# A Mamba branch beside a two-layer local-attention branch on one core: dt by one Softplus activation, and the rotary addition by an accumulating DMA that GpSimd issues

## The reference, cut to what matters

```python
def mamba(x):                                     # 512 inner channels, 16 states
    x_inner, z = split(x @ in_proj_w.T)
    x_conv = silu(causal_conv4(x_inner) + conv_b)
    dt_lr, B, C = split(x_conv @ x_proj_w.T)
    dt = softplus(dt_lr @ dt_proj_w.T + dt_proj_b)
    h_t = exp(dt_t * A) * h_(t-1) + (dt_t * x_conv_t) * B_t      # per channel and state
    y_t = sum_n h_t[n] * C_t[n] + x_conv_t * D
    return (y * silu(z)) @ out_proj_w.T

def attention_layer(x, l):                        # 2 layers, 8 heads of 64, windows of 128
    q, k, v = split(shift_token(x) @ wqkv[l])
    q, k = l2norm(q) * q_scale, l2norm(k) * k_scale
    q = q * cos * scale + rotate_half(q) * sin * scale
    k = k * cos / scale + rotate_half(k) * sin / scale
    x = x + local_attention(q, k, v) @ wo[l]
    return x + gelu_feed_forward(layernorm(shift_token(x)))
```

## Time and profile before

| | |
|---|---|
| median of 3 runs | 2244.7 us (2244.4 to 2245.45) |
| the profiled execution | 2240.7 us, its span 2238.9 us |
| PE busy | 2058.0 us (92%) |
| DVE busy | 2016.8 us (90%) |
| ACT busy | 1680.9 us (75%) |
| POOL busy | 928.2 us (41%) |
| DMA queues, share of 16 engines | q0 36.0%, q1 31.4% |
| mean granted TensorE clock | 0.976 |

### The profile page before, as it was taken

One profiled execution on the slowest core, in us unless ns is written; L12 is line 12 of the kernel. 1 busy time (PEld: TensorE's weight loads), 2 busy tenths in 40 slices (PEclk: granted clock), 3 DMA queues, 4 the chain that ended last, 5 costly groups with the idle time before them and its releaser, 6 DMA issues. The chain is left out here.

```text
span 2238.9 us, 37820 instructions
## 1 busy us (share of the span) xinstructions
PE 2058.0 (92%) x10944; PEld 1318.1 (59%) x10944; DVE 2016.8 (90%) x2804; ACT 1680.9 (75%) x4087; POOL 928.2 (41%) x1086
## 2 busy tenths in 40 slices
PE   6789989999899999999899998999989999898897
PEld 2355666656566566665566565666556656565565
DVE  2999989999899999999899998999989999899893
ACT  3777877968778787887778777787777868778682
POOL 2444343444434444443444433444443443533440
PEclk9889999999999999999999999999999999999999
DMA  4567767686676756877756876668667686667482
GB/s 142 145 152 194 188 155 183 180 205 175 161 196 178 188 161 157 220 187 169 193 136 189 208 187 165 157 179 200 181 166 196 173 197 167 163 162 217 115 200 54
DMA packets 113131, 388.52 MB, mean 174 GB/s; under 512 B 11408, under 2 KB 32272, under 8 KB 94368
## 3 DMA queue, kind: packets, MB, share of 16 engines
q0 software_dynamic: 46080, 151.02, 36.0%
q1 hardware_dynamic: 66848, 235.10, 31.4%
HBM read 238.75 MB, written 155.71 MB: 176 GB/s over the span
## 5 line engine op out<-in xcount | busy, mean ns | idle before, releaser
L756 DVE TENSOR_TENSOR_SCAN hb<-dA,state,hb 128x512 f32<-128x512 f32 x512 | 668.3, 1305 | 34.7 <-ACT dA L963 20.5
L1177 POOL COPY state<-hb 128x2 f32<-128x2 f32 x256 | 223.5, 873 | 638.5 <-DVE hb L756 638.2
L963 ACT ACTIVATE dA<-dt_sb,amat 128x512 f32<-128x512 f32 x512 | 344.3, 720 | 81.8 <-DMA ysum<-dA 80.8
L1193 POOL DMA_DIRECT2D ysum<-dA x256 | 220.2, 883 | 382.6 <-DVE dA L763 272.6
L1465 PE MATMUL ring<-hT,w 128*128 128x256 f32 (+1 forms) x1536 | 354.5, 388 | 17.4 <-ACT hT L1119 16.9
L1465 PEld LDWEIGHTS ring<-hT,w 128*128 128x128 f32 (+1 forms) x1536 | 272.6, 182 | 94.5 <-ACT hT L1119 26.0
L749 DVE TENSOR_TENSOR hb<-u_sb,bc 128x1024 f32<-128x1024 f32 x256 | 311.3, 1216 | 2.0 <-DMA bc<-bc_rows 1.9
L763 DVE TENSOR_TENSOR dA<-hb,bc 128x1024 f32<-128x1024 f32 x256 | 307.2, 1200 | 0.0
L1073 ACT ACTIVATE rot<-rot,rnorm 128x64 f32<-128x64 f32 x1024 | 257.2, 339 | 50.8 <-POOL rnorm L1262 50.7
L1098 ACT ACTIVATE probs<-ring,nmax 128x256 f32<-128x256 f32 x512 | 235.6, 483 | 55.5 <-DVE nmax L847 55.1
L1262 POOL TENSOR_TENSOR rnorm<-rnorm,powers 128x8 f32<-128x8 f32 x128 | 230.2, 1799 | 23.5 <-POOL rnorm L1259 23.5
(11 more groups left out here) (122 smaller groups left out, 3469.8 us busy)
## 6 DMA issues: line engine op xcount, KB each, us to landing
bc<-bc_rows SPq DMA_DIRECT2D x128, 1024.0 KB, 5.8
ysum<-dA POOLq DMA_DIRECT2D x256, 512.0 KB, 7.2
wqkv<-in_wqkv SPq DMA_DIRECT2D x48, 512.0 KB, 8.6
w<-in_w SPq DMA_DIRECT2D x16, 1364.0 KB, 9.5
...
wo<-in_wo SPq DMA_DIRECT2D x16, 512.0 KB, 10.0
...
```

Source lines behind the costliest of these rows:

```text
L756: dve.tensor_tensor_scan(hb[:, k % H_RING, :], dA[:, k % DA_RING, :], hb[:, k % H_RING, :], state[:, k:k + 1], ALU.mult, ALU.add).then_inc ...
L963: act.activation(dA[:, k % DA_RING, :], dt_sb[:, j, :], ACT.Exp, scale=amat[:, n:n + 1]).then_inc(dA_ready.sem, 1)
```

## The change

dt: the three activations and two VectorE operations become one activation, `Softplus`, from PSUM with the bias, straight into `dt_sb`; `clip` and `softplus(half)` are gone, and `u(half)` has only its product. The rotation: VectorE's addition at line 842 is gone, and a new stage `rot` on POOL issues a DMA from `sq` to `rot` (both in SBUF, 128 partitions by 2 KB, 256 KB) that adds to the destination. `norm_heads` and the next `square` wait for its landing. All order tables are written anew for it, of which two lines are shown.

```diff
 POOL_ORDER = """
...
-+scan +scan +turn(q,1) +q(2) +add(2) +add(3) +scan +scan +turn(k,1) +add(4) +add(5) +scan +add(6) +scan
...
+stats(3) +scan +skip(0) +scan +turn(q,1) +turn(k,1) +add(2) +scan +add(3) +scan +rot(q,1) +rot(k,1) +scan
...
-    rot_ready = Signal("rot_ready", 2 * NA)
+    rot_added = [Signal(f"rot_added_{x}", D16 * NA, primed=0) for x in "qk"]
...
             elif stage == "dt":
-                group(("dt", n[0]), (dtv_ready, n[0] + 1))
+                group(("dt", n[0]), (dt_ready, n[0] + 1))
...
-            def clip(half):
-                for j in range(half * JH, half * JH + JH):
-                    dve.wait_ge(*dtv_ready.at(it, j + 1))
-                    dve.wait_ge(*dBx_ready.at(it - 1, (half + 1) * SUMS // HALVES))
-                    dve.tensor_scalar(u_sb[:, j, :], dt_sb[:, j, :], 40.0, None, ALU.min).then_inc(dtmin_ready.sem, 1)
-
             def u(half):
 
-                for j in range(half * JH, half * JH + JH):
-                    dve.wait_ge(*dtlog_ready.at(it, j + 1))
-                    dve.tensor_tensor(dt_sb[:, j, :], dt_sb[:, j, :], u_sb[:, j, :], ALU.max)\
-                       .then_inc(dt_ready.sem, 1)
                 for j in range(half * JH, half * JH + JH):
                     dve.wait_ge(*dt_ready.at(it, j + 1))
                     dve.wait_ge(*xconv_ready.at(it, j + 1))
+                    dve.wait_ge(*dBx_ready.at(it - 1, (half + 1) * SUMS // HALVES))
                     dve.tensor_tensor(u_sb[:, j, :], dt_sb[:, j, :], xconv[:, j, :], ALU.mult).then_inc(u_ready.sem, 1)
...
-                dve.wait_ge(*sine_ready.at(it, n + 1))
-                dve.wait_ge(*rotary_ready.at(it, n + 1))
-                dve.tensor_tensor(rot[:, i, :], rot[:, i, :], sq[:, i, :], ALU.add).then_inc(rot_ready.sem, 1)
...
-            def dt_out(j):
+            def softplus(j):
                 act.wait_ge(*filled(it, ("dt", j)))
                 act.wait_ge(*dA_ready.at(it - 1, (j // JH + 1) * UNITS // HALVES))
-                act.activation(dt_sb[:, j, :], bank(it, ("dt", j))[:, :], ACT.Identity,
-                               bias=par[:, C_DTB + j:C_DTB + j + 1]).then_inc(dtv_ready.sem, 1)
-
-            def softplus(half):
-                act.preload_act_table_set("natural_log_exp_and_others")
-                for j in range(half * JH, half * JH + JH):
-                    act.wait_ge(*dtmin_ready.at(it, j + 1))
-                    act.activation(u_sb[:, j, :], u_sb[:, j, :], ACT.Exp).then_inc(dtexp_ready.sem, 1)
-                for j in range(half * JH, half * JH + JH):
-                    act.wait_ge(*dtexp_ready.at(it, j + 1))
-                    act.activation(u_sb[:, j, :], u_sb[:, j, :], ACT.Ln, bias=1.0).then_inc(dtlog_ready.sem, 1)
+                act.activation(dt_sb[:, j, :], bank(it, ("dt", j))[:, :], ACT.Softplus,
+                               bias=par[:, C_DTB + j:C_DTB + j + 1]).then_inc(dt_ready.sem, 1)
 
             def square(i, name, a):
                 n = 2 * a + i
-                act.wait_ge(*rot_ready.at(it, n - 1))
+                if it or a:
+                    act.wait_ge(*rot_added[i].at(it, D16 * a))
                 act.wait_ge(*filled(it, (name, a)))
                 act.activation(sq[:, i, :], bank(it, (name, a))[:, :], ACT.Square).then_inc(sq_ready.sem, 1)
...
-                act.wait_ge(*rot_ready.at(it, n + 1))
+                act.wait_ge(*rot_added[i].at(it, D16 * (a + 1)))
                 act.wait_ge(*rnorm_ready.at(it, n + 1))
...
+            def add_rotated(name, a):
+
+                i = "qk".index(name)
+                n = 2 * a + i
+                pool.wait_ge(*sine_ready.at(it, n + 1))
+                pool.wait_ge(*rotary_ready.at(it, n + 1))
+                pool.sem_inc(passed, 1)
+                pool.dma_start(rot[:, i, :], sq[:, i, :], accum_op=ALU.add).then_inc(rot_added[i].sem, D16)
+
```

More of the change, by code:

```diff
@@ L120 @@
++e(5,2) +e(5,3) +k(6) +dA +dA +dA +dA +pT(5,0) +pT(5,1) +v(5) +rb(5) +pT(5,2) +pT(5,3) +turn(q,6) +turn(k,6)
++dA +dA +heads(6) +v(6) +q(7) +hn(2) +e(6,0) +e(6,1) +hT(2) +e(6,2) +e(6,3) +last(2) +k(7) +pT(6,0)
+++skip(0) +dA +dA +pT(6,1) +dA +dA +dA +h(2,0) +h(2,1) +h(2,2) +h(2,3) +rb(6) +h(2,4) +h(2,5) +pT(6,2)
++pT(6,3) +turn(q,7) +turn(k,7) ++dA ++dA
 """
 POOL_ORDER = """
-add(30) add(31) scan +scan merge(1) +turn(q,0) +turn(k,0) +scan +q(1) +add(0) +add(1) stats(3) +skip(0)
-+scan +scan +turn(q,1) +q(2) +add(2) +add(3) +scan +scan +turn(k,1) +add(4) +add(5) +scan +add(6) +scan
@@ L175 @@
-e(5,2) e(5,3) v(5) rb(4) dA q(6) dA k(6) pT(5,0) pT(5,1) pT(5,2) pT(5,3) +softplus(0) rb(5) turn(q,6)
-turn(k,6) last(2) heads(6) v(6) dA dA dA dA e(6,0) e(6,1) hn(2) e(6,2) pT(6,0) e(6,3) q(7) pT(6,1) hT(2)
-pT(6,2) k(7) turn(q,7) h(2,0) h(2,1) dA dA pT(6,3) h(2,2) h(2,3) h(2,4) h(2,5) dA dA +dA +dA turn(k,7)
-+skip(0) rb(6)
+xn(0) xnT(0) start(0) xn(1) q(0) xnT(1) in(0) k(0) in(1) start(1) turn(q,0) +xn(0) in(2) in(3) turn(k,0)
+silu(0) silu(1) xdbl heads(0) v(0) dt(0) dt(1) dt(2) dA e(0,0) q(1) k(1) dA dA e(0,1) e(0,2) dA dA dA e(0,3)
@@ new lines @@
+pT(3,0) dA dA dA x2T(0) +in(1) +in(2) pT(3,1) pT(3,2) q(4) dA pT(3,3) dA dA +in(3) k(4) rb(3) +silu(0) dA dA
+turn(q,4) dA dA turn(k,4) hn(1) dA hT(1) +silu(1) q(5) k(5) heads(4) dA dA dA dA last(1) h(1,0) h(1,1)
+h(1,2) h(1,3) h(1,4) h(1,5) e(4,0) e(4,1) dA dA dA +xdbl pT(4,0) turn(q,5) dA +dt(0) +dt(1) pT(4,1)
+turn(k,5) v(4) dA heads(5) dA e(4,2) e(4,3) dA dA pT(4,2) x2T(1) e(5,0) e(5,1) e(5,2) e(5,3) q(6) k(6)
+pT(4,3) dA dA rb(4) v(5) pT(5,0) pT(5,1) pT(5,2) pT(5,3) rb(5) turn(q,6) turn(k,6) heads(6) dA dA e(6,0)
@@ new lines @@
+turn(k,2) add(2) scan scan add(3) add(4) scan add(5) scan q(3) add(6) add(7) rot(q,3) rot(k,3) scan
+turn(q,3) turn(k,3) add(8) stats(0) scan scan carry add(9) add(10) scan add(11) scan scan add(12) add(13)
++halo scan q(4) scan add(14) add(15) scan add(16) turn(q,4) add(17) rot(q,4) scan rot(k,4) merge(0)
+turn(k,4) skip(1) scan stats(1) q(5) scan scan add(18) add(19) add(20) add(21) rot(q,5) rot(k,5) scan scan
+turn(q,5) +tail turn(k,5) q(6) add(22) scan scan add(23) add(24) scan scan rot(q,6) rot(k,6) turn(q,6)
@@ L188 @@
+turn(k,6) add(25) add(26) q(7) stats(2) scan scan add(27) add(28) turn(q,7) scan rot(q,7) turn(k,7) rot(k,7)
+scan carry2 add(29) +q(0)
 """
 SP_FIRST = """
-x(0) x(1) w2(0) wol(0) +x(0) +x(1) xdbl v(0) v(1) q(0) w1(0) bc(0) q(1) bc(1) bc(2) k(0) bc(3) k(1) bc(4)
-k(2) bc(5) k(3) v(2) bc(6) bc(7) bc(8) v(3) v(4) q(2) q(3) bc(9) bc(10) q(4) k(4) xres(0) bc(11) +xdbl
-bc(12) y(0) v(5) w1(1) bc(13) q(5) q(6) wol(1) bc(14) w2(1) k(5) v(6) k(6) bc(15) +bc(0) v(7) q(7) +q(0)
-k(7) +v(0) +k(0)
+x(0) x(1) +x(0) k(0) +x(1) k(1) xdbl w1(0) wol(0) w2(0) bc(0) bc(1) bc(2) bc(3) k(2) q(0) q(1) bc(4) q(2)
@@ L246 @@
++v(6) +e(6,0) +e(6,1) +hn(2) +q(7) +pT(6,0) +e(6,2) +pT(6,1) +e(6,3) +k(7) +hT(2) +dA +last(2) +pT(6,2) +dA
++dA +dA +pT(6,3) +dA +h(2,0) +h(2,1) +h(2,2) +turn(q,7) +turn(k,7) +h(2,3) +h(2,4) +h(2,5) +heads(7) +dA +dA
++rb(6) +e(7,0) +e(7,1) +v(7) +e(7,2) +e(7,3) +rb(7) +pT(7,0) +pT(7,1) +pT(7,2) +pT(7,3) +hn(3) +hT(3)
++h(3,0) +h(3,1) +h(3,2) +h(3,3) +h(3,4) +last(3) +h(3,5)
 """
 POOL_LAST = """
-scan add(30) +scan add(31) +add(0) +turn(q,0) +turn(k,0) +q(1) +scan merge(1) +add(1) stats(3) +turn(q,1)
@@ new lines @@
++add(9) +scan +q(3) +q(4) +rot(q,3) +rot(k,3) +scan +add(10) +turn(q,3) +turn(k,3) +stats(0) +add(11) +scan
++scan +add(12) +add(13) +add(14) +scan +scan +scan +carry +add(15) +add(16) +turn(q,4) +rot(q,4) +add(17)
++scan +rot(k,4) +scan +turn(k,4) +skip(1) +q(5) +stats(1) +scan +add(18) +add(19) +rot(q,5) +scan +scan
++rot(k,5) +add(20) +add(21) +turn(q,5) +turn(k,5) +scan +scan +add(22) +add(23) +add(24) +q(6) +scan
++rot(q,6) +turn(q,6) +rot(k,6) +turn(k,6) +scan +scan +add(25) +merge(0) +add(26) +stats(2) +scan +q(7)
```

308 lines of the change are left out of this document (144 added, 164 removed).

## The result

The changed kernel is slower: **2322.6 us**, median of 4 runs (2317.5 to 2335.8), against 2244.6 for the kernel before in 4 runs beside it (2242.8 to 2245.5). The ratio is 1.036, with a 95% interval of 1.031 to 1.040. The forecast was 2200, its range ended at 2250, and slower had a chance of 0.14.

What follows compares the result with a forecast made beforehand. PE and DVE, both near 94% busy, were taken to lose time where in-order lists wait for each other. The terms -9 - 8 - 26 - 14 + 12 gave -45 us from 2240.7: 2195.7, or 2200 as run median, range 2165 to 2250.

Steps and rivals of the forecast that it cites:

- The landing of 4.7 us: Time for the rotation's transfer to land, taken from line 1210's median; range to 10.8 left open.
- the 12 us for the rotation: PE's added waits for the later rotation: 1.5 us a pass and 2 at the end, 12 us lost.
- The close places: Steps 0, 2, 4 and 6 of a pass, where the rotation's landing has least room; PE waits 1 to 2 us at k(0).
- the signs written down for being wrong: Landings of 7 us and more with waits, period 265 or above with a new 3 us wait, or POOL too late.
- Rival B: The rotation's landing decides and the kernel gets slower: landing 8.3 us, 10.6 us a pass lost, 2274 us; chance 0.13.
- the 45 us of gains: The forecast's sum over all terms, -45 us, which rival B's 2274 also subtracts.
- All of this is off the path, except at the start: ACT's savings from Softplus and 13 fewer loads gain nothing but at the start; ACT had over 59 us a pass to spare.
- the 8 us: Gain in the first pass, from chunk 0's shorter dt chain and less DVE work: 8 us, bounds 0 and 20.
- The `qT` wait: PE's wait at `heads(7)` for ACT's `qT`: 26 of 30.4 us go, with 14 of 16 us of slow clock.
- DVE, 9 us: VectorE loses 126.3 us of work, 235.5 us a pass; PE waits less for it, 1.5 us a pass, 9 us.
- 8% more queue time and 16 us a pass on GpSimd: Load of the new transfers: 33.6 MB more on queue q0, and 16 issues a pass on POOL.

Runs made afterwards that it cites:

- r4: The changed kernel with the load `xres(1)` moved three places up in SyncE's order, ahead of bc(3): 2284.6 us, 1.018.
- r7: `r4` with each addition into `ysum` moving 256 of its 1024 columns, the others left out of y: 2197.0 us, 0.978.
- r3: The kernel before with the rotation's accumulating DMA alone, each issued right behind its power on GpSimd: 2535.8 us, 1.132.
- r11: `r4` with four issues of the rotation a pass moved forward in GpSimd's list: 2257.7 us, 1.006.
- r1x: The changed kernel with the rotation's addition back on VectorE, no transfer of it, and `xres(1)` early: 2270.9 us, 1.011.
- r1: The changed kernel with the rotation's addition back on VectorE and the new DMA gone: 2271.7 us, 1.013.
- r2: The kernel before with Softplus alone, in place of the copy out of PSUM, all else in its old order: 2273.5 us, 1.013.
- r9: The kernel before with the copy kept and Softplus where Exp and Ln stood, minimum and maximum gone: 2235.4 us, 0.997.
- r13: The kernel before with ScalarE's copies `heads(7)` moved ahead of the two `dA` that wait for transfers: 2233.2 us, 0.992.
- r10: `r4` with VectorE adding and the same 256 KB also sent to a spare DRAM tensor, no rotation waiting for it: 2294.0 us, 1.023.

## Why the prediction was wrong

- **The landing of 4.7 us, and the 12 us for the rotation made from it: the step that failed.** The landing is 7.6 us at the median, and PE's wait for the rotation went from 15.3 us over the span to 83.1, 68 more, where the forecast had 1 to 2 us a pass. Line 1210's transfers, the row I took the 4.7 from, were the wrong neighbour. They leave in pairs as the rotations do, but 8.9 and 5.2 us behind the last 512 KB addition (issued at 857.63 and 1003.87, the additions at 848.71 and 998.63); in `r4` the rotations of step 1 leave 3.5 us behind one and 5.2 behind another. That this distance is what differs is argued; that the additions ahead matter, `r7` shows. In the old order (`r3`), behind the powers, the transfer does land in 4.2 us; behind the changed order's additions in 7.3; with those additions a quarter as large, in 5.4.
- **The issue, missing from the same term.** I had charged the landing from the moment VectorE is done. At step 1 (`r4`) GpSimd's list held the issue back by 15 us more, which no term had: I counted GpSimd's issues as busy time and did not walk its list for what stands ahead of each. That is 27 us by `r11`. The close places were not the forecast ones either: PE waits at `heads(2)`, `heads(3)` and `heads(6)` in the pass from 1086.75, and not at `heads(0)`, which I had worked through, or `heads(4)`. Two of the signs written down for being wrong came true: landings of 7 us and more with PE and ACT waiting for them, and a period above 265.
- **Rival B is the nearest to what happened**, with its turning point: "from a median landing of about 7 us". Its 2274 is close to what the changed kernel takes once the late load is out, 2284.6 (`r4`), but partly by luck: it still counts the 45 us of gains, which did not come. `r1x` also limits it, since 24 us of loss are there with no transfer at all. Its chance of 0.13 was too small, since the very row against it came from a lighter moment of the queue.
- **SyncE's list: a step that was missing.** `xres(1)` behind `+wol(0) +k(1)`, and `out(0)` later on TensorE, were costed by no term. 38 us, half of the loss (by `r4`; with the addition on VectorE, `r1` to `r1x`, the same move gave nothing that can be told apart). The kernel before had 0.5 us of waits for `xres` in the whole span, so there was no row that warned; the order of the two programs did.
- **"All of this is off the path, except at the start": wrong.** The price of the activation was right (0.68 us forecast as 0.69), the count of loads too, and both were added up over the span where only one place mattered. `r2` loses 30 us with 5.1 us of loads at one point of a pass. The Trainium skill's page "ScalarE: Activation LUTs", section "Rules for kernel authors", asks for exp and ln from one set; I set that aside because the lists held fewer loads in all. `r2` sides with the rule, `r9` shows that it is the place that decides. Of the 2.66 us for a switch in its section "What ACT_TABLE_LOAD costs" these traces show the 1.28 us of the load alone. At the start the 8 us did not come either: the first stretch is 8 us longer.
- **The `qT` wait: right in mechanism, too large.** The wait went as forecast, 25 of its 30.4 us; 26 + 14 us were written for it, and removed by itself it gives 17 (`r13`). The next in line, the copy of V, waited 18.7 us there.
- **DVE, 9 us:** `r9` takes 26.7 us off VectorE and gains 6.6, about a quarter. It can't be told apart in the changed kernel, where VectorE is at 83% and TensorE waits all the same. The sum of the rows was too large as busy time: 126 us were forecast and 98 went, 239.3 us a pass and not 235.5. The addition's row has 88.7 us, and from `r1x` to `r4` VectorE's busy time fell by 72; the rows of the minimum and the maximum have 37.6, and `r9` shows the 26.7.
- **What the sum lacked as a whole** is what a transfer costs the others: 23 to 27 us by `r10`, when no rotation waits for it, by its traffic and by GpSimd's time for the issues. I had noted 8% more queue time and 16 us a pass on GpSimd and given them no price.

The 78 us, then: 38 the late load, 27 the late issues, and 13 left in `r11`, the net of the remaining landings, the traffic, GpSimd's issues, Softplus, the other new orders, and the gains. No run takes these 13 apart.
